# Rows and gates in two tables, ten gathers per expert, and a new order of the first expert's blocks

## The chip, the cores and the metric

The kernel runs on one core of a Trainium2 chip. The metric is the device time of one launch in microseconds (us); lower is better. The core's engines run side by side: TensorE (PE, matrix products), VectorE (DVE), ScalarE (ACT), GpSimd (POOL) and SyncE (SP, which issues transfers). They meet only at semaphores: an instruction waits until a counter has reached a value. POOL issues the indirect transfers (gathers and scatters), SP the plain ones.

## The reference

One transformer block with modulated layer norms, linear attention, and a mixture of eight experts, two per token. Cut to the part that the change touches:

```python
xf = x.reshape(-1, D)                       # N = 4096 tokens, D = 256
probs = softmax(xf @ router_w.T)            # E = 8 experts
topw, topi = top_k(probs, 2)                # normalised weights
# the best 640 tokens of each expert (capacity = 1.25 * N / E), by weight
disp = zeros((E, 641, D)).at[se, pos].set(xf[st])[:, :640]
g = einsum('ecd,edf->ecf', disp, wg)        # F = 1024
u = einsum('ecd,edf->ecf', disp, wu)
eo = einsum('ecf,efd->ecd', silu(g) * u, wd)
out = zeros_like(xf).at[st].add(eo[...] * weight)
y = x + gb * out                            # gb: one gate row per batch
```

## The kernel before

Attention comes first (to about 210 us); it leaves a table `h2_rows` in device memory. A row of it belongs to one token and holds 256 numbers that go into the experts, 256 gate numbers, and 8 expert weights: 520 numbers, 2080 bytes. Then the tokens of each expert are chosen by counting.

Each expert has 640 slots, five tiles of 128. `gather(e, par)` (POOL, L553) issues five indirect transfers, one per tile, each of which brings 128 whole rows into `xg[par]`. PE transposes the first 256 numbers of the tiles in three groups: tiles 0 and 1, tile 2, tiles 3 and 4 (`transpose_x(e, par, g)`, L1577; it waits for the group's gathers, `ga_d`). ACT casts each transposed group to `xT_h` (`x_high`, L711), DVE makes the rest `xT_l` (`x_low`, L1226), since every product is done in three passes of a high and a low part.

The hidden dimension is cut in eight blocks f. `gate_up(e, par, f)` (L1603) does two halves h of 320 slots; each half is 12 matmuls into two banks, six for the gate product (m=0) and six for the up product (m=1). Half h=0 needs the first two groups of tokens, half h=1 all three. After each half four steps follow: ACT `act_g` (silu, L729), DVE `hid` (product, L1258), ACT `hid_h` (L733), DVE `hid_l` (L1263). `down(e, f)` (L1624) takes both halves of `hid_h` and `hid_l` back through 15 matmuls into banks 4 to 6. PE's order is gate_up(f), down(f-1), so that the four steps hide behind one block. A half may overwrite its banks once `hid` of the half before has been formed (`hid_d`).

Weights: SP loads an expert's raw weights in two halves of the blocks (`load_weights`, L366; f below 4 is `raw_a`, the others `raw_b`); ACT casts them (`split_high`, L701) and DVE takes the rest (`split_low`, L1213), block by block, during the expert before. `raw_b` of expert e+1 is issued only when the first token group of e+1 has been transposed (`trx_d`, L449).

Beside this, DVE finds the tokens of the next expert: `describe_blocks`, `describe_facts`, `describe_rows` build tables of zeros and ones from the slots (`place_slots`, L1137); PE's `look(e)` (L1563) and DVE's `find_diagonal` (L1184), PE's `place(e)` (L1572) and DVE's `find_tokens` (L1193) give the indices `g_idx`, upon which POOL gathers. After its last `down` an expert's results are weighed (`weigh`, L1239, uses the gate numbers and weights in `xg`) and scattered with addition (`scatter`, L561).

The orders of all engines are written out by hand. For the first expert (e = 0) they differ: PE runs both halves of f=0, then both of f=1, with the third token group's transposes between the gate and the up product of the first half (L1620); `look(1)` stands ahead of `down(0, 0)`, `place(1)` in f=2. Expert 1's three token groups are transposed after gate_up of f=5, 6 and 7, while in the other experts it is f=4, 5 and 6 (`xf`, L1676). On DVE `place_slots(1)` stands ahead of the first `x_low`, and the description of expert 1 in block f=0.

Of the kernel before, what the change touches and what calls it, by code (L numbers as in the profile page):

```python
# [16 lines left out]
P = 128  # L17
F32, F32R = mybir.dt.float32, mybir.dt.float32r
BF16, I32, U32 = mybir.dt.bfloat16, mybir.dt.int32, mybir.dt.uint32
ALU = mybir.AluOpType  # L20
ACT = mybir.ActivationFunctionType
# [6 lines left out]
N = B * T  # L28
# [109 lines left out]
def build_program(nc, x, w_qkv, w_out, router, wg, wu, wd, c, wmod, rope, consts, out):  # L138
# [3 lines left out]
    h2_rows = nc.dram_tensor("h2_rows", (N, 2 * D + E), F32, kind="Internal").ap()  # L142
    h2_t = h2_rows[:, 0:D].rearrange("(n p) d -> n p d", p=P)
    gate_t = h2_rows[:, D:2 * D].rearrange("(b n p) d -> b p n d", b=B, p=P)
    w_t = h2_rows[:, 2 * D:].rearrange("(n p) e -> p n e", p=P)
# [3 lines left out]
    with ExitStack() as ctx:  # L149
# [3 lines left out]
        def sem(name):  # L153
            return ctx.enter_context(nc.semaphore(name))
# [189 lines left out]
        ga_d = [sem(f"ga_d{g}") for g in range(XG)]  # L344
# [120 lines left out]
        def _(pool):  # L465
# [87 lines left out]
            def gather(e, par):  # L553

                for a in range(CT):
                    nc.gpsimd.indirect_dma_start(  # L556
                        out=xg[par][:, a, :], out_offset=None, in_=h2_rows,
                        in_offset=bass.IndirectOffsetOnAxis(ap=g_idx[par][:, a:a + 1], axis=0))\
                        .then_inc(ga_d[next(g for g, t in enumerate(ROW_GROUPS) if a in t)], 16)

# [33 lines left out]
        def _(act):  # L594
# [123 lines left out]
            for g in range(XG):  # L718
                x_high(0, 0, g, bk=(0, 1, 7)[g])

            def expert(e, par, first=False):
                xf = FC - XG if first else XF
                for f in range(FC):
                    for h in range(2):
                        i = e * 2 * FC + 2 * f + h
                        wait(act, gu_d, i + 1)
                        if f or not first:
                            wait(act, hid_d, i - 1)
                        nc.scalar.activation(act_g[h][:, 0:HCAP], bank[2 * h][:, 0:HCAP], ACT.Silu).then_inc(silu_d, 1)  # L729
                        wait(act, hid_d, i + 1)  # L730
                        if f >= 2 or not first:
                            wait(act, dn_d, e * FC + f - 1)
                        nc.scalar.copy(hid_h[f % 2][:, h * HCAP:(h + 1) * HCAP], hid[h][:, 0:HCAP]).then_inc(hh_d, 1)  # L733
                    if xf <= f < xf + XG:
                        x_high(e + 1, 1 - par, f - xf)
                    if f < 2:

                        split_high(e, FC - 2 + f, e * FC + FC - 2 + f, implied=True)
                    else:
                        split_high(e + 1, f - 2, e * FC + FC + f - 2)  # L740
# [25 lines left out]
        def _(dve):  # L766
# [426 lines left out]
            def find_tokens(e, par):  # L1193

                dve.wait_ge(place_d, e + 1)
                TT(spot[:, :].rearrange("p (m q) -> p m q", q=Q),
                   bank[7][:, Q * BAND:(Q + 1) * BAND].rearrange("p (m q) -> p m q", q=Q),
                   own_q[:, :].unsqueeze(1).to_broadcast([P, BAND // Q, Q]), ALU.mult).then_inc(spot_d, 1)
                dve.wait_ge(spot_d, e + 1)
                with nc.allow_low_precision(reason="row numbers under 4096 are whole and exact"):  # L1200
                    RED(g_idx[par][:, :], spot[:, :].rearrange("p (v a q) -> p a v q", v=NV, q=Q), AXY, ALU.add)\  # L1201
                        .then_inc(idx_d, 1)
# [5 lines left out]
            def find_weights(e, par):  # L1208

                dve.wait_ge(trx_d, e * XG + XG)  # L1210
                V.tensor_copy(w_slot[par][:, :], xg[par][:, :, 2 * D + e]).then_inc(ws_d, 1)
# [21 lines left out]
            place_slots(1)  # L1233
            x_low(0, 0, 0, bk=0)
            x_low(0, 0, 1, bk=1)
            split_low(0, 4, 4)
            x_low(0, 0, 2, bk=7)
# [12 lines left out]

            def expert(e, par, first=False, ahead=True):

                def hidden(f, h):
                    i = e * 2 * FC + 2 * f + h
                    wait(dve, silu_d, i + 1)
                    if f or not first:
                        wait(dve, hh_d, i - 1)
                    V.tensor_tensor(hid[h][:, 0:HCAP], act_g[h][:, 0:HCAP], bank[2 * h + 1][:, 0:HCAP], ALU.mult)\  # L1258
                        .then_inc(hid_d, 1)
# [16 lines left out]
                xf = FC - XG if first else XF  # L1276
                for f in range(FC):
                    hidden(f, 0)
                    if f == 0 and first:
                        describe_blocks(1)  # L1280
                        describe_facts(1, 0)
                    if f == 0 and not first:
                        weigh(e - 1, 1 - par, 0, 2)
                    if f == (3 if first else 1):
                        find_tokens(e + 1, 1 - par)
# [6 lines left out]
                    if f == 0 and first:  # L1292
                        describe_facts(1, 1)
                        describe_rows(1, 0)
                        describe_rows(1, 1)
                    if f == 0 and not first:
                        weigh(e - 1, 1 - par, 2)
                    if f == 4:
                        find_weights(e, par)
                    hidden_low(f, 1)  # L1300
                    if f == 0 and first:
                        split_low(0, 5, 5)
# [6 lines left out]
                    if f == 1 and first:  # L1309
                        find_diagonal(1)  # L1310
# [15 lines left out]
            def last_expert(e, par):  # L1326

                for j in range(2 * FC):
# [9 lines left out]
                    if j == 4:  # L1338
                        find_weights(e, par)
                        dve.wait_ge(ws_d, e + 1)  # L1340
# [19 lines left out]
        def _(pe):  # L1360
# [242 lines left out]
            def gate_up(e, par, f, first=False):  # L1603
                W, XT = (w_h, w_l), (xT_h[par], xT_l[par])
                wait(pe, sp_l, e * FC + f + 1)
                for h in range(2):
                    if f == 0:
                        wait(pe, xl_d, e * XG + XG - 1 + h)
                    if f or not first:
                        wait(pe, hid_d, e * 2 * FC + 2 * f + h - 1)  # L1610
                    cols = slice(h * HCAP, (h + 1) * HCAP)
                    for m in range(2):
# [7 lines left out]
                        if first and (h, m) == (0, 0):  # L1620
                            transpose_x(0, 0, XG - 1, first=True)
                    last.then_inc(gu_d, 1)

            def down(e, f):  # L1624
                wait(pe, hh_d, e * 2 * FC + 2 * f + 2)
                wait(pe, hl_d, e * 2 * FC + 2 * f + 2)
# [48 lines left out]
            def expert(e, par, first=False, ahead=True, then_last=False):  # L1675
                xf = FC - XG if first else XF  # L1676
                for f in range(2, FC):
                    gate_up(e, par, f)
                    if f == 2 and first:
                        place(1)  # L1680
                    if xf <= f < xf + XG:
                        transpose_x(e + 1, 1 - par, f - xf)
                    down(e, f - 1)
                    if f == FC - 1 and ahead:
                        wait(pe, xl_d, e * XG + 2 * XG)
                        look(e + 2)
# [11 lines left out]
            gate_up(0, 0, 0, first=True)  # L1698
            gate_up(0, 0, 1)
            pe.wait_ge(idx_d, 1)  # L1700
            look(1)
            down(0, 0)
# [64 lines left out]
```

## Time and profile before

| | us |
|---|---|
| runs shown: median of 3 (lowest to highest) | 629.87 (627.71 to 632.21) |
| the profiled execution | 629.0 |
| its span, first to last instruction | 627.3 |
| PE busy | 583.7 (93%) |
| DVE busy | 452.5 (72%) |
| ACT busy | 320.4 (51%) |
| POOL busy | 269.8 (43%) |

The profiled execution took 629.0 us, of which 627.3 are the span that the trace shows and 1.7 lie around it. Attention fills the trace to about 210 us, the choice of tokens to about 246, the eight experts the rest. The mean granted clock of PE over the span was 0.993 of full speed. In the timelines a row is one instruction, or several alike ("x2"), with its start, its length, and in brackets the time that the engine stood idle before it and whom it had waited for. Matmuls overlap: one of 320 columns starts every 0.147 us or so though each is shown as 0.31 long, so lengths of a row of them are read from start to start.

### The profile page before, as it was taken

To read this page: it belongs to the slowest core of one execution; us is meant where nothing else is said; L and a number is where in the kernel's file an instruction comes from. 1 tells how busy PE (TensorE), PEld (TensorE's weight loads), DVE (VectorE), ACT (ScalarE), POOL (GpSimd) and SP (SyncE) were. 2 spreads that over 40 slices of the span, in tenths; PEclk is the share of its full clock that TensorE was granted. 3 is DMA by queue.
4 is the path that set the end of the run, shared out by engine and by line. 5 is a ranking of instruction groups with operands and counts; after the bars stand their busy time and mean duration, and the time that the engine had idled before them with its cause. 6 is when DMAs were issued, how large, how long until landed. Compare 5 with 4: busy or idle time off the path is not lost.

```text
span 627.3 us, 13151 instructions
## 1 busy us (share of the span) xinstructions
PE 583.7 (93%) x4013; PEld 527.4 (84%) x4013; DVE 452.5 (72%) x1357; ACT 320.4 (51%) x718; POOL 269.8 (43%) x406
## 2 busy tenths in 40 slices
PE   5999999999899778799899999999999999999993
PEld 4587779988787333599899999999999999999993
DVE  4688899998899888787567667666776775566441
ACT  4688878886444433244436445445444454354331
POOL 5788857776778302212061080170260440521321
PEclk9999999999999999899999999999999999999998
DMA  6322468644665730505356167066174373450312
GB/s 173 102 67 85 119 178 249 216 137 143 199 195 177 234 86 17 170 15 168 106 106 169 57 119 211 17 124 187 49 145 133 76 152 103 101 128 8 36 19 25
DMA packets 92482, 75.29 MB, mean 120 GB/s; under 512 B 12157, under 2 KB 89095, under 8 KB 92425
## 3 DMA queue, kind: packets, MB, share of 16 engines
q1 hardware_dynamic: 82344, 57.39, 30.7%
q0 software_dynamic: 8992, 15.90, 13.8%
q10 hardware_dynamic: 1088, 1.31, 0.7%
q8 instruction: 28, 0.46, 0.3%
q14 instruction: 30, 0.24, 0.1%
HBM read 52.41 MB, written 22.16 MB: 119 GB/s over the span
## 4 chain that ended last, share of the span: by engine, by line
PE 64%; DVE 9%; issue 4%; ACT 3%; DMA 3%; POOL 2%; SPq 1%; another core or an unknown queue 1%; POOLq 0%; ACTq 0%; DVEq 0%
PE bank L1617 29%; PE bank L1631 14%; PE bank L1652 4%; PE bank L1384 4%; PE bank L1509 4%; DVE hit L1075 2%; PE bank L1667 2%; PE bank L1495 2%; PE bank L1587 1%; PE bank L1421 1%; DMA q_in<-q_store 1%; DMA w_raw<-wd 1%; POOL xg L556 1%; PE bank L1464 1%
## 5 line engine op out<-in xcount | busy, mean ns | idle before, releaser
L556 POOL DMA_INDIRECT xg<-h_rows,g_idx x40 | 44.2, 1105 | 239.3 <-DVE g_idx L1201 229.5
L1617 PE MATMUL bank<-xT_h,w_h 128*128 128x320 f32 x448 | 140.5, 314 | 1.9 <-DVE hid L1258 0.9
L1617 PE MATMUL bank<-xT_l,w_h 128*128 128x320 f32 x448 | 138.6, 309 | 0.0
L1617 PE MATMUL bank<-xT_h,w_l 128*128 128x320 f32 x448 | 138.4, 309 | 0.0
L733 ACT CAST hid_h<-hid 128x320 fp32r<-128x320 f32 x112 | 51.5, 460 | 91.0 <-DVE hid L1258 83.6
L566 POOL DMA_INDIRECT out<-yo,s_idx x40 | 66.7, 1668 | 62.0 <-DVE yo L1323 26.6
L1617 PEld LDWEIGHTS bank<-xT_h,w_h 128*128 128x128 f32 x448 | 84.8, 189 | 3.6 <-issue 1.8
L729 ACT ACTIVATE act_g<-bank 128x320 f32<-128x320 f32 x112 | 48.9, 436 | 72.4 <-PE bank L1617 61.4
L1617 PEld LDWEIGHTS bank<-xT_l,w_h 128*128 128x128 f32 x448 | 84.7, 189 | 0.0
L1617 PEld LDWEIGHTS bank<-xT_h,w_l 128*128 128x128 f32 x448 | 84.6, 189 | 0.0
L1258 DVE TENSOR_TENSOR hid<-act_g,bank 128x320 f32<-128x320 f32 x112 | 54.2, 484 | 41.5 <-ACT act_g L729 38.2
L1263 DVE TENSOR_TENSOR hid_l<-hid,hid_h 128x320 fp32r<-128x320 f32 x112 | 54.8, 490 | 37.8 <-ACT hid_h L733 37.4
L1631 PE MATMUL bank<-w_h,hid_h 128*128 128x256 f32 x280 | 80.2, 286 | 0.0
L1631 PE MATMUL bank<-w_h,hid_l 128*128 128x256 f32 x280 | 78.3, 280 | 0.3 <-issue 0.3
L1631 PE MATMUL bank<-w_l,hid_h 128*128 128x256 f32 x280 | 78.3, 280 | 0.0
L1216 DVE TENSOR_TENSOR w_l<-w_raw,w_h 128x768 fp32r<-128x768 f32 x64 | 61.1, 960 | 11.4 <-ACT w_h L706 10.9
L706 ACT CAST w_h<-w_raw 128x768 fp32r<-128x768 f32 x64 | 52.8, 832 | 2.5 <-DMA w_raw<-wd 2.5
L1631 PEld LDWEIGHTS bank<-w_h,hid_l 128*128 128x128 f32 x280 | 52.8, 189 | 0.6 <-issue 0.5
L1631 PEld LDWEIGHTS bank<-w_l,hid_h 128*128 128x128 f32 x280 | 52.8, 189 | 0.2
L1384 PE MATMUL bank<-wqkv_h,hT_h 128*128 128x256 f32 (+1 forms) x128 | 49.2, 384 | 4.1 <-DVE hT_l L968 2.5
L1631 PEld LDWEIGHTS bank<-w_h,hid_h 128*128 128x128 f32 x280 | 52.7, 188 | 0.1
L542 POOL TENSOR_TENSOR rot<-rot_a,rot_b 128x512 f32<-128x512 f32 x32 | 42.3, 1321 | 11.3 <-DVE rot_b L961 10.7
(225 smaller groups left out, 1330.1 us busy)
## 6 DMA issues: line engine op xcount, KB each, us to landing
w_raw<-wg SPq DMA_DIRECT2D x32, 256.0 KB, 3.4
w_raw<-wu SPq DMA_DIRECT2D x32, 256.0 KB, 4.8
w_raw<-wd SPq DMA_DIRECT2D x16, 512.0 KB, 5.8
x_in<-x SPq DMA_DIRECT2D x32, 128.0 KB, 2.2
q_store<-qT SPq DMA_DIRECT2D x32, 128.0 KB, 2.2
q_in<-q_store SPq DMA_DIRECT2D x32, 128.0 KB, 2.3
x_re<-x SPq DMA_DIRECT2D x32, 128.0 KB, 2.1
out<-x SPq DMA_DIRECT2D x32, 128.0 KB, 2.1
```

The costliest lines, as they stand in the source:

```text
L542: nc.gpsimd.tensor_tensor(rot[s.par(0)][:, :], rot_a[:, :], rot_b[:, :], ALU.add).then_inc(rope_d, 1)
L556: nc.gpsimd.indirect_dma_start(out=xg[par][:, a, :], out_offset=None, in_=h2_rows, in_offset=bass.IndirectOffsetOnAxis(ap=g_idx[par][:, a: ...
L566: nc.gpsimd.indirect_dma_start(out=out_rows, out_offset=bass.IndirectOffsetOnAxis(ap=s_idx[par][:, a:a + 1], axis=0), in_=yo[:, a, :], in_ ...
L706: nc.scalar.copy(w_h[:, f, :], w_raw[:, f, :]).then_inc(sp_h, 1)
L729: nc.scalar.activation(act_g[h][:, 0:HCAP], bank[2 * h][:, 0:HCAP], ACT.Silu).then_inc(silu_d, 1)
L733: nc.scalar.copy(hid_h[f % 2][:, h * HCAP:(h + 1) * HCAP], hid[h][:, 0:HCAP]).then_inc(hh_d, 1)
L1216: V.tensor_tensor(w_l[:, f, :], w_raw[:, f, :], w_h[:, f, :].bitcast(F32), ALU.subtract).then_inc(sp_l, 1)
L1258: V.tensor_tensor(hid[h][:, 0:HCAP], act_g[h][:, 0:HCAP], bank[2 * h + 1][:, 0:HCAP], ALU.mult)\
L1263: V.tensor_tensor(hid_l[f % 2][:, h * HCAP:(h + 1) * HCAP], hid[h][:, 0:HCAP], hid_h[f % 2][:, h * HCAP:(h + 1) * HCAP].bitcast(F32), ALU. ...
L1384: ins = MM(out, x[j][:, k, :], w[i][:, k, cols], start=n == 0, stop=n == 3 * KC - 1)
L1617: last = MM(bank[2 * h + m][:, 0:HCAP], W[i][:, f, at:at + P], XT[j][:, k, cols], start=n == 0, stop=n == 3 * KC - 1)
L1631: last = MM(bank[4 + a // 2][:, a % 2 * D:(a % 2 + 1) * D], (hid_h, hid_l)[j][f % 2][:, a * P:(a + 1) * P], (w_h, w_l)[i][:, f, 4 * P:], s ...
```

## The change

1. The table is split: `h2_rows` keeps the 256 token numbers (1024 bytes a row), a new `g_rows` takes gates and weights (1056 bytes a row).
2. `gather` issues ten transfers: five for the token rows, which count `ga_d` as before, then five for gates and weights, which count a new `ga_rest`. `find_tokens(e)` waits until the gathers of all experts before e have landed whole; `find_weights` loses its wait.
3. The first expert opens in another order of half-blocks: (f=0, h=0), (f=1, h=0), (f=0, h=1), (f=1, h=1). The third token group is transposed in the middle of the second of them. `down(0, 0)` waits for three pieces.
4. ACT's and DVE's orders for the opening follow: DVE does two `x_low` ahead of `place_slots(1)`, and the description of expert 1 is spread between the steps; the splits of the expert's last four weight blocks come behind it.
5. In expert 0 `look(1)` moves from ahead of `down(0, 0)` to behind gate_up of f=2, `place(1)` to f=3, `find_tokens(1)` from the first to the second half of f=3 on DVE, `find_diagonal(1)` from f=1 to f=2. Expert 1's token groups are transposed at f=4, 5, 6, behind `down(f-1)` and not ahead of it.

```diff
-    h2_rows = nc.dram_tensor("h2_rows", (N, 2 * D + E), F32, kind="Internal").ap()
+    h2_rows = nc.dram_tensor("h2_rows", (N, D), F32, kind="Internal").ap()
+    g_rows = nc.dram_tensor("g_rows", (N, D + E), F32, kind="Internal").ap()
...
                 for a in range(CT):
                     nc.gpsimd.indirect_dma_start(
-                        out=xg[par][:, a, :], out_offset=None, in_=h2_rows,
+                        out=xg[par][:, a, 0:D], out_offset=None, in_=h2_rows,
...
+                for a in range(CT):
+                    nc.gpsimd.indirect_dma_start(
+                        out=xg[par][:, a, D:], out_offset=None, in_=g_rows,
+                        in_offset=bass.IndirectOffsetOnAxis(ap=g_idx[par][:, a:a + 1], axis=0)).then_inc(ga_rest, 16)
...   ACT
-            for g in range(XG):
-                x_high(0, 0, g, bk=(0, 1, 7)[g])
+            x_high(0, 0, 0, bk=0)
+            x_high(0, 0, 1, bk=1)
+            opening_silu(0)
+            x_high(0, 0, 2, bk=7)
+            opening_high(0)
+            opening_silu(1)
+            opening_high(1)
+            split_high(0, FC - 2, FC - 2, implied=True)
+            opening_silu(2)
+            opening_high(2)
+            opening_silu(3)
+            opening_high(3)
+            split_high(0, FC - 1, FC - 1, implied=True)
...   DVE
             def find_tokens(e, par):
+                wait(dve, ga_rest, e * CT * 16)
                 dve.wait_ge(place_d, e + 1)
...
             def find_weights(e, par):
-                dve.wait_ge(trx_d, e * XG + XG)
...
-            place_slots(1)
             x_low(0, 0, 0, bk=0)
             x_low(0, 0, 1, bk=1)
-            split_low(0, 4, 4)
-            x_low(0, 0, 2, bk=7)
+            place_slots(1)
...
+            opening(0)
+            describe_blocks(1)
+            x_low(0, 0, 2, bk=7)
+            opening_low(0)
+            opening(1)
+            describe_facts(1, 0)
+            opening_low(1)
+            opening(2)
+            opening_low(2)
+            opening(3)
+            opening_low(3)
+            describe_facts(1, 1)
+            describe_rows(1, 0)
+            describe_rows(1, 1)
+            split_low(0, 4, 4)
+            split_low(0, 5, 5)
...   PE
+            def opening(j):
+                f, h = j % 2, j // 2
+                pe.wait_ge(sp_l, f + 1)
+                pe.wait_ge(xl_d, XG - 1 + h)
+                if j >= 2:
+                    pe.wait_ge(hid_d, j - 1)
+                for m in range(2):
...
+                    if (j, m) == (1, 0):
+                        transpose_x(0, 0, XG - 1, first=True)
...
             def expert(e, par, first=False, ahead=True, then_last=False):
-                xf = FC - XG if first else XF
+                xf = XF
                 for f in range(2, FC):
                     gate_up(e, par, f)
                     if f == 2 and first:
+                        pe.wait_ge(idx_d, 1)
+                        look(1)
+                    if f == 3 and first:
                         place(1)
-                    if xf <= f < xf + XG:
+                    if xf <= f < xf + XG and not first:
                         transpose_x(e + 1, 1 - par, f - xf)
                     down(e, f - 1)
+                    if xf <= f < xf + XG and first:
+                        transpose_x(e + 1, 1 - par, f - xf)
...
-            gate_up(0, 0, 0, first=True)
-            gate_up(0, 0, 1)
-            pe.wait_ge(idx_d, 1)
-            look(1)
-            down(0, 0)
+            for j in range(4):
+                opening(j)
+            down(0, 0, pieces=3)
             expert(0, 0, first=True)
```

## Rows read from the trace of the kernel before

**Rows 1.** Timeline of PE, first expert: start us, us, instruction, idle before and releaser
```profile
254.49 0.44 PE L1587 MATMUL bank<-const_sb,xg 128*128 128x128 f32 x2 [0.73 <-DMA xg<-h_rows,g_idx]
...
255.94 0.39 PE L1617 MATMUL bank<-xT_h,w_h 128*128 128x320 f32 x1 [0.36 <-DVE xT_l L1230]
...
258.51 0.66 PE L1587 MATMUL bank<-const_sb,xg 128*128 128x128 f32 x4 [1.45 <-DMA xg<-h_rows,g_idx]
...
260.57 0.64 PE L1617 MATMUL bank<-xT_h,w_h 128*128 128x320 f32 x1 [0.52 <-DVE xT_l L1230]
...
263.92 0.31 PE L1617 MATMUL bank<-xT_h,w_h 128*128 128x320 f32 x1
...
273.94 0.19 PE L1575 MATMUL bank<-diag,same_r 128*128 128x40 bf16 x1 [0.45 <-DVE diag L1191]
...
305.37 0.73 PE L1568 MATMUL bank<-facts,onehot 128*128 128x160 bf16 x8 [1.94 <-DVE xT_l L1230]
305.89 0.39 PE L1617 MATMUL bank<-xT_h,w_h 128*128 128x320 f32 x1
```

**Rows 2.** Busy time by window: window, us, engines' busy us, granted clock, DMA share, GB/s
```profile
262.00:264.00 2.00, 2.00 (x10) 2.00 (x9) 1.32 (x3) 0.00 (x0) 0.00 (x0) 0.53 0.82 236
```

**Rows 3.** The chain that ended last, first expert: start us, us, what
```profile
275.99 3.51 PE bank L1617 x24
279.51 1.73 PE bank L1631 x15
...
289.99 0.45 PE bank L1587 x4
```

**Rows 4.** Timeline of ACT, columns as for PE
```profile
254.97 0.37 ACT L715 CAST xT_h<-bank 128x256 fp32r<-128x256 f32 x1 [0.79 <-PE bank L1587]
...
299.98 0.83 ACT L706 CAST w_h<-w_raw 128x768 fp32r<-128x768 f32 x1 [2.49 <-DMA w_raw<-wd]
```

**Rows 5.** Timeline of POOL, gathers of experts 0 and 1
```profile
250.72 1.42 POOL L556 DMA_INDIRECT xg<-h_rows,g_idx  x1 [0.30 <-issue]
...
253.69 1.13 POOL L556 DMA_INDIRECT xg<-h_rows,g_idx  x1 [0.30 <-issue]
279.36 1.28 POOL L556 DMA_INDIRECT xg<-h_rows,g_idx  x1 [24.53 <-DVE g_idx L1201]
```

**Rows 6.** Timeline of DVE, opening and description of expert 1
```profile
254.77 1.02 DVE L1230 TENSOR_TENSOR xT_l<-bank,xT_h 128x512 fp32r<-128x512 f32 x2
...
260.96 0.17 DVE L1155 TENSOR_SCALAR block_no<-slot 128x32 int32<-128x32 int32 x1
...
262.10 0.82 DVE L1167 TENSOR_TENSOR facts<-vals,in_block 128x640 bf16<-128x640 bf16 x1
...
265.73 1.29 DVE L1175 TENSOR_TENSOR onehot<-iota_s,row_in 128x512 bf16<-128x512 bf16 x2
...
267.33 1.82 DVE L1216 TENSOR_TENSOR w_l<-w_raw,w_h 128x768 fp32r<-128x768 f32 x2
...
273.11 0.32 DVE L1187 TENSOR_TENSOR band<-bank,own_q 128x160 f32<-128x160 f32 x1
...
278.90 0.20 DVE L1201 TENSOR_REDUCE g_idx<-spot 128x5 int32<-128x40 f32 x1
```

**Rows 7.** The page's costliest groups: line, operation, count | busy us, mean ns | idle before
```profile
L1263 DVE TENSOR_TENSOR hid_l<-hid,hid_h 128x320 fp32r<-128x320 f32 x112 | 54.8, 490 | 37.8 <-ACT hid_h L733 37.4
```

**Rows 8.** Timeline of SP's queue, the load of expert 2's second half
```profile
331.84 0.93 SPq L377 DMA_DIRECT2D w_raw<-wg  x2
```

**Rows 9.** Timeline of POOL in expert 1: the last transfer of its scatter
```profile
330.35 2.29 POOL L566 DMA_INDIRECT out<-yo,s_idx  x1 [0.30 <-issue]
```

**Rows 10.** Timeline of ACT in expert 1: the cast that needs that load
```profile
344.28 0.83 ACT L706 CAST w_h<-w_raw 128x768 fp32r<-128x768 f32 x1
```

**Rows 11.** Busy time by window, quiet ahead of the gathers and behind that load
```profile
226.00:228.00 2.00, 1.54 (x9) 0.59 (x7) 1.78 (x13) 0.60 (x2) 0.00 (x0) 1.00 0.00 0
...
339.00:340.00 1.00, 1.00 (x9) 1.00 (x8) 0.81 (x3) 0.76 (x2) 0.00 (x0) 1.00 0.19 62
```

## What the change does to the time: the prediction

> **What bounds the kernel now.** I read the page's busy times first: PE is busy for 93% of the span, so a change counts only where it takes idle or slow time out of PE's path, or puts some in. Then the chain that ended last: from the first expert on it is almost all PE, gate_up and down in turn, a block of 3.51 us and a down of 1.73 [rows 3]. Then the waits of PE: in experts 1 to 6 it hardly stops, so the change can win only in the opening and in expert 0, which it reorders. There the timeline shows where PE stood [rows 1]: 1.45 us for the gathers of the third token group, 0.52 for its `x_low`, 0.45 for the diagonal of expert 1, and 1.94 at the end for the last `x_low` of expert 1. In between ran 12 matmuls at half clock: from 260.57 to 263.92 they took 3.35 us where half a block takes 1.76, 1.6 too many; the granted clock of 262 to 264 reads 0.53 [rows 2], that is 1.2 GHz, after PE had done little from 257 to 260.5 [rows 1]. The 1.94 has a cause further back: the load of expert 1's second weight half is issued behind the transposes that end at 290.44 [rows 3], its data end ACT's 2.49 us wait at 299.98 [rows 4], and the last `x_low` stands behind all that.
>
> Accounting: the first opening matmul starts at 255.94, that of expert 1 at 305.89 [rows 1], 49.95 us. The work in it is 8 blocks and 7 downs, 40.2, three groups of four transposes and one of two (0.45 and 0.22), 1.6, two looks of 0.52 and a place of 0.1, 1.1: together 42.9. The other 7.05 us are stops and slow clock. What the change is worth is how much of them it leaves.
>
> **The change, walked through.** I lay the new orders on the durations of before, in the clock of its trace.
>
> Start. The second `x_low` ended at 255.79 [rows 6], since `place_slots` (1.6 us) ran ahead of it. Now it follows its cast, which ended at 255.34 [rows 4], by about 0.42: PE starts at 255.8 if the rows land as before. They should land sooner, since each gather brings half the bytes. The third gather's issue ended at 252.14 and its transposes began 2.35 us later; the fifth ended at 254.82 and its began 3.69 later [rows 1, 5]: the last wait behind the bytes of the others. With 1024 of 2080 bytes the 2.35 lies between 1.16 (all of it goes with the bytes) and 2.35 (none does); halfway gives 0.6 less, but the matmuls between the transposes hide some. I take 255.6, bounds 255.3 and 255.8. The Trainium skill, "DMA: Bandwidth & Descriptors" (Anatomy of one DMA), gives a fixed 2.0 us and bytes over 436 GB/s for such a transfer. By that estimate a gather of 128 rows goes from 2.6 to 2.3 us, and the start would be 255.5. The third gather's 2.35 agrees with the size of it.
>
> First two half-blocks. From 255.6 half (0, 0) runs to 257.36, the gate product of (1, 0) to 258.24. The last token rows should have landed at 254.82 + 2.35 = 257.2, at worst at 258.51 as before: no wait, at worst 0.3. Transposes 0.45, up product 0.88: 259.6. So the 1.45 goes.
>
> Third half. In before it was 2.06 us from the start of those transposes to the matmul that needs them (258.51 to 260.57 [rows 1]). Now from 258.24: 260.3, and 0.05 for `describe_blocks` (1.14 us, 260.96 to 262.10 [rows 6]), which DVE runs just ahead of that `x_low`. PE waits 0.75 us, in place of 0.52. But it has been at work since 255.6 with no other gap, so I let the clock stay at full speed. Two halves to 263.85.
>
> `down(0, 0)` needs three pieces through all four steps. The third half ends at 262.1; four steps of 0.49 at most [rows 7] and their hand-overs make 2.1, and ACT's cast of weight block 6 may add 0.1: 264.35, a new wait of 0.5. In before `look(1)` and block 1 hid it. Then down to 266.1, block 2 to 269.6, look 270.1, down(1) 271.85, block 3 275.35.
>
> Diagonal. DVE now carries more ahead of `find_diagonal(1)`. The fourth half ends at 263.85, and its low part is done on DVE at 265.9. Behind it follow a half of the facts (0.74), both rows (1.20) and two splits (1.74), each read from start to start, 0.08 less than its row [rows 6]: 269.6. Then product 0.41, split 0.87, `describe_blocks(2)` 1.14, low part and product 0.82: 272.8; a cast on ACT to wait for, 0.5, low part 0.4, two splits 1.74: 275.5. From the diagonal's first instruction to `place` it was 0.83 [rows 1, 6]: 276.35. PE comes to `place(1)` at 275.35 and waits 1.0, in place of 0.45; behind it in PE's queue stand down(2) and all later blocks. That is the change's largest new cost.
>
> Expert 1's gather. place, down(2), block 4, down(3): 283.5. DVE needs product, facts, targets, low part and product (2.05 us) from 276.25 before `find_tokens`, 0.43: indices at 278.75. POOL starts 0.26 later (279.10 to 279.36 [rows 5, 6]), two gathers take 1.28, 0.30 and 1.13: 281.7. With 1.2 to 2.35 for landing the first group is there between 282.9 and 284.1, PE asks at 283.5: a wait of 0 to 0.6, I take 0.3.
>
> The rest. From 283.8 four transposes, block 5, down(4), two transposes, block 6, down(5), four transposes, block 7, down(6) and look: 17.35, which gives 301.15 for expert 1's first matmul. The load of the second weight half goes out at 284.3, 6 us sooner; counted with the same 9.4 us that it took before (to 299.98, beside another load) it is there at 293.7, and ACT's cast of it is due behind block 6 at about 295. So the 2.49 and the 1.94 go, also because the last `x_low` now stands in f=6.
>
> **What costs nothing.** Stores into two tables: they move the same bytes, and the transfers are quiet from 226 [rows 11], 20 us before the first gather; without that cover the gathers would wait for them. The waits on `ga_rest` are for gathers of the expert before, issued most of a block sequence earlier. Five more POOL issues of 1.13 + 0.30 [rows 5] are 7.1 us an expert. Behind them stand the five scatters, and for these waits `weigh`, seven blocks of 5.24 us, 36 us, later. The gate rows are needed there too.
>
> **Sum.** 305.89 - 301.15 = 4.7 us: 0.3 at the start, and 7.05 us of stops cut to some 2.6 (0.75, 0.5, 1.0, 0.3). On the profiled execution's 629.0 (627.3 of span and 1.7 around it) this gives 624.3. That execution was 0.9 under the median of the runs, 629.87, from which it would be 625.2. I predict 624.7. Bounds: all the small costs at their worse ends (start 0.2, gather 0.3, transposes 0.3) leave 3.9; all new waits at nothing give 7.2, but the diagonal's 1.0 is a sum of DVE's own work and hardly goes.
>
> **Rivals.**
> - The clock falls all the same. PE has gaps at 254 to 255.6 and at 259.6; if it falls there, 12 matmuls again cost 1.6. For it speaks that in before a wait of similar size stood in just this stretch [rows 1, 2]; against it, that the 1.45 before it is gone. With rows that land no sooner, the gain is 2.3 to 3.1: 626.5. Chance 0.18.
> - More is won: the rows land fast enough to bring the start to 255.3, the wait for expert 1's rows is none, and DVE overtakes part of the diagonal's delay. Gain 5.5 to 7: 622.7. Chance 0.14.
> - Slower: scatters run into the weight loads. In expert 1 the last scatter's issue ends at 332.64 [rows 9], and the load of expert 2's second half is issued at 331.84 [rows 8], so the two hardly meet. With 7.1 us more of gathers all of the scatter's second half runs beside the load, in each of six experts. The load is over by 339.8 [rows 11] and its cast starts at 344.28 [rows 10], 4.5 us of cover; then cast, low part and product (2.2 us) must be ready for PE's next expert, which comes one block and one down after block 6, about 4 us more. So it decides once the load is 8 us longer, twice its length; beyond that each us is paid six times. At 2 us each the gain turns into 12 - 4.7 = 7.3 us of loss: 636.3. The Trainium skill, "DMA: Bandwidth & Descriptors" (Rules for kernel authors), would have many small transfers coalesced into one large, which speaks against ten gathers in place of five. The cover in these rows is why I give it little. Chance 0.06.
>
> **How the numbers follow.** The forecast has 0.62 (gain 3.5 to 5.5, so 623.5 to 626.4 from the one base or the other). The range takes in the clock's case and most of the better one: 621.9 to 627.6, and leaves out some 0.15. A measurement of this kernel, whose runs spread from 627.71 to 632.21, can tell about 1%, 6.3 us, from no change. Faster by more than that needs a gain over 6.3: the better case's upper half and chance in the runs, 0.16. Slower over 1%: 0.05. Within: 0.79.
>
> **What would show it.** Of the new profile: gathers of experts show ten POOL issues with the first group's transposes after shorter landings; the granted clock from 260 to 264 at 1.0; PE's waits in expert 0 are `x_low` 0.75, `hid_l` 0.5 ahead of the first down, `diag` 1.0, rows of expert 1 up to 0.6, and no 1.94 at the end; expert 1's first matmul near 301; ACT waits for no weights at f=6. A clock at half speed, a longer `diag` or row wait, or PE waiting for `hid` in experts 1 to 6 behind late weights would make it wrong.

## The result, and the profile after

The changed kernel is slower: 659.6 us (median of 6 runs, 657.79 to 673.03) against 628.49 for the kernel before on the same chip, a ratio of 1.049 (95% interval 1.0455 to 1.0526). Ratios, here and below, are of fast executions alone: those over 1.5% above the fastest of the same kernel (here the one of 673.03) are in the medians but not in the ratios. The profiled execution took 658.09 us, its span 656.2. The forecast was 624.7, with 627.6 as its upper end.

First the page's busy times and PE's granted clock:

```profile
PE 597.5 (91%) x4013; PEld 535.8 (82%) x4013; DVE 453.3 (69%) x1357; ACT 320.9 (49%) x718; POOL 310.0 (47%) x446
...
PEclk9999999999999999999979989989999989979999
```

POOL has the 40 transfers more that the change gives it, and 40 us of work more. PE's work is the same 4013 matmuls but 13.8 us longer: in the second half the granted clock dips five times, in experts 1, 2, 3, 5 and 6. Its slices read 7 or 8 there, where before they stood at 9 until the end.

Then each expert's length, from its first gate activation on ACT's timeline to the next expert's: before, experts 0 to 6 took 47.9, 44.3, 44.4, 44.4, 44.4, 43.8, 45.5 us; after, 48.3, 52.5, 49.9, 50.0, 48.4, 48.5, 50.9. Experts 1 to 6 lost 33.6 us. All else together won 4.6: the way from the first gather to expert 1's first activation 2.15 (61.16 to 59.01), the last expert 1.0, the end of the program 2.2; only the first gather came 0.8 later.

What stands in those experts? Busy time by window, for one expert of before and the same of after (us, busy us of PE, PEld, DVE, ACT, POOL with their instructions, granted clock, DMA share, GB/s):

```profile
352.30:396.70 44.40, 44.24 (x333) 43.94 (x332) 30.66 (x61) 21.09 (x44) 13.81 (x10) 1.00 0.50 117
```

```profile
359.13:409.03 49.90, 46.38 (x333) 45.43 (x332) 30.84 (x61) 21.31 (x43) 18.98 (x15) 0.97 0.43 104
```

Of 5.5 us more, 3.4 are idle time of PE (3.52 after, 0.16 before) and 2.1 go to the same matmuls, at a lower clock. The DMA engines are less busy than before, so they are not the bound. The timeline of that stretch shows the stop itself:

```profile
369.31 0.31 PE L1690 MATMUL bank<-xT_h,w_l 128*128 128x320 f32 x1
...
369.65 0.44 ACT L757 ACTIVATE act_g<-bank 128x320 f32<-128x320 f32 x1 [0.98 <-PE bank L1690]
...
372.94 0.83 ACT L711 CAST w_h<-w_raw 128x768 fp32r<-128x768 f32 x1
...
374.01 1.57 POOL L562 DMA_INDIRECT xg<-g_rows,g_idx  x1 [0.31 <-issue]
...
374.55 0.31 PE L1690 MATMUL bank<-xT_h,w_l 128*128 128x320 f32 x1
...
379.00 0.44 ACT L757 ACTIVATE act_g<-bank 128x320 f32<-128x320 f32 x1 [5.24 <-remote]
379.47 0.49 DVE L1314 TENSOR_TENSOR hid<-act_g,bank 128x320 f32<-128x320 f32 x1 [4.72 <-ACT act_g L757]
...
380.02 0.42 PE L1690 MATMUL bank<-xT_h,w_h 128*128 128x320 f32 x1 [1.67 <-issue]
...
381.84 0.32 PE L1690 MATMUL bank<-xT_h,w_h 128*128 128x320 f32 x1 [0.24 <-issue]
...
382.56 0.41 PE L1690 MATMUL bank<-xT_h,w_l 128*128 128x320 f32 x1 [0.24 <-issue]
```

The matmul at 374.55 is the last of a half-block. It ends by the profile at 374.86, and the silu that needs only this half starts at 379.00, 4.1 us late. One block earlier the hand-over took 0.03: the matmul ends at 369.62, the silu starts at 369.65. The trace's list of semaphore rises has this rise at 378.98, while those of ACT and DVE in the same stretch stand 0.01 behind their instructions. So PE's completion is told late, ACT and DVE stand, and at 380.02 PE runs out of finished hidden parts. The end of a matmul is modelled, so the trace alone does not show whether the work itself was late or only the word of it; the 27 matmuls behind this one, to 378.07, start at their usual distance. From 381.3 PE itself only creeps, a pair of matmuls and then a hole. In expert 1 the same creeping goes on for 7 us: the matmuls of a `down`, which wait for nothing that the profile shows ("issue"), start in ones and twos some 0.7 us apart.

```profile
325.55 0.28 PE L1702 MATMUL bank<-w_l,hid_h 128*128 128x256 f32 x1 [1.11 <-issue]
325.67 0.28 PE L1702 MATMUL bank<-w_h,hid_h 128*128 128x256 f32 x1
326.27 0.28 PE L1702 MATMUL bank<-w_h,hid_l 128*128 128x256 f32 x1 [0.33 <-issue]
326.39 0.28 PE L1702 MATMUL bank<-w_l,hid_h 128*128 128x256 f32 x1
326.99 0.37 PE L1702 MATMUL bank<-w_h,hid_h 128*128 128x256 f32 x1 [0.33 <-issue]
```

The busy times of the creeping and of what follows it, at half clock:

```profile
324.00:331.30 7.30, 3.38 (x17) 2.22 (x15) 0.35 (x1) 0.00 (x0) 5.82 (x5) 0.90 0.42 91
331.30:337.00 5.70, 4.65 (x18) 4.65 (x19) 3.15 (x7) 2.86 (x6) 4.79 (x4) 0.53 0.64 73
```

In the view of waits many of these late hand-overs are put down to "remote", since no instruction ends near them. First the kernel before, then the changed one (engine, what waits, releaser: us in total, times, longest; from 300 us on):

```profile
ACT act_g L729 <- remote: 9.5, 3, 5.1
```

```profile
ACT act_g L757 <- remote: 40.1, 11, 8.0
```

The kernel before has three of that name, each while its five gathers or the scatters behind ran; this is the longest:

```profile
549.08 0.44 ACT L729 ACTIVATE act_g<-bank 128x320 f32<-128x320 f32 x1 [5.06 <-remote]
```

PE did not wait for them, and so they were in none of the rows that the prediction was built on. The view does not name them all. If a hand-over is called late where the silu starts more than 0.6 us behind both the last matmul's end and ACT's own work before it, the timelines have ten in the kernel before, up to 4.0 us, and twenty in the changed one, up to 8.0 us.

### The profile page after: what moved, and what is told of

The parts are those of the page before. It is cut to its first block, busy times and chain, and to the rows that moved or that the text cites. A ratio compares the mean times of both kernels' runs of the same rounds, so it can differ in the third digit from the quotient of the medians.

```text
span 656.2 us, 13200 instructions
## 1 busy us (share of the span) xinstructions
PE 597.5 (91%) x4013; PEld 535.8 (82%) x4013; DVE 453.3 (69%) x1357; ACT 320.9 (49%) x718; POOL 310.0 (47%) x446
## 4 chain that ended last, share of the span: by engine, by line
PE 60%; DVE 11%; issue 9%; ACT 3%; DMA 2%; POOL 1%; another core or an unknown queue 0%; POOLq 0%; SPq 0%; DVEq 0%; ACTq 0%
PE bank L1690 27%; PE bank L1702 13%; PE bank L1723 4%; PE bank L1563 4%; PE bank L1438 2%; DVE hit L1102 2%; PE bank L1738 2%; PE bank L1641 1%; PE bank L1549 1%; DMA x_in<-x 1%; PE bank L1670 1%; DVE hid L1314 1%; PE bank L1475 1%; DVE w_l L1243 1%; PE bank L1573 1%
## 5 line engine op out<-in xcount | busy, mean ns | idle before, releaser
L1690 PE MATMUL bank<-xT_h,w_h 128*128 128x320 f32 x432 | 139.1, 322 | 17.3 <-DVE hid L1314 10.1
L1690 PE MATMUL bank<-xT_h,w_l 128*128 128x320 f32 x432 | 136.4, 316 | 0.8 <-issue 0.8
L1690 PE MATMUL bank<-xT_l,w_h 128*128 128x320 f32 x432 | 136.6, 316 | 0.1
L1314 DVE TENSOR_TENSOR hid<-act_g,bank 128x320 f32<-128x320 f32 x108 | 52.3, 485 | 72.9 <-ACT act_g L757 49.9
L757 ACT ACTIVATE act_g<-bank 128x320 f32<-128x320 f32 x108 | 47.2, 437 | 105.0 <-PE bank L1690 59.9
L760 ACT CAST hid_h<-hid 128x320 fp32r<-128x320 f32 x108 | 49.6, 460 | 87.2 <-DVE hid L1314 78.9
L571 POOL DMA_INDIRECT out<-yo,s_idx x40 | 64.1, 1604 | 59.2 <-DVE yo L1376 25.7
L1319 DVE TENSOR_TENSOR hid_l<-hid,hid_h 128x320 fp32r<-128x320 f32 x108 | 52.9, 490 | 36.1 <-ACT hid_h L760 33.3
L1702 PEld LDWEIGHTS bank<-w_h,hid_h 128*128 128x128 f32 x280 | 53.1, 190 | 1.7 <-issue 1.0
L562 POOL DMA_INDIRECT xg<-g_rows,g_idx x40 | 43.3, 1082 | 12.2 <-issue 12.2
```

Of the source, the lines that this page charges most:

```text
L562: nc.gpsimd.indirect_dma_start(out=xg[par][:, a, D:], out_offset=None, in_=g_rows, in_offset=bass.IndirectOffsetOnAxis(ap=g_idx[par][:, a: ...
L571: nc.gpsimd.indirect_dma_start(out=out_rows, out_offset=bass.IndirectOffsetOnAxis(ap=s_idx[par][:, a:a + 1], axis=0), in_=yo[:, a, :], in_ ...
L1319: V.tensor_tensor(hid_l[f % 2][:, h * HCAP:(h + 1) * HCAP], hid[h][:, 0:HCAP], hid_h[f % 2][:, h * HCAP:(h + 1) * HCAP].bitcast(F32), ALU. ...
L1690: last = MM(bank[2 * h + m][:, 0:HCAP], W[i][:, f, at:at + P], XT[j][:, k, cols], start=n == 0, stop=n == 3 * KC - 1)
L1702: last = MM(bank[4 + a // 2][:, a % 2 * D:(a % 2 + 1) * D], (hid_h, hid_l)[j][f % 2][:, a * P:(a + 1) * P], (w_h, w_l)[i][:, f, 4 * P:], s ...
```

## Experiments: which part, which place, which distance

Fifteen kernels, in order. "Ratio" is that of the runs to those of the kernel before on the same chip, with its 95% interval (the median is that of all runs; the kernel before had 626.0 to 628.5 on the chips used); an expert's length is taken as above, from the profiled execution.

| run | median us | ratio | expert 0 | experts 1 to 5, mean |
|---|---|---|---|---|
| kernel before | 628.49 | | 47.9 | 44.3 |
| changed kernel | 659.6 | 1.049 (1.0455 to 1.0526) | 48.3 | 49.9 |
| e1_order_only | 625.49 | 0.998 (0.9954 to 0.9998) | 46.3 | 44.1 |
| e2_tables_only | 638.5 | 1.020 (1.0157 to 1.0236) | 46.7 | 45.8 |
| e3_gates_last | 625.93 | 0.998 (0.9953 to 1.0012) | 53.1 | 44.1 |
| e4_gates_late | 625.2 | 0.996 (0.993 to 0.9987) | 49.6 | 44.0 |
| e5_paced | 618.45 | 0.984 (0.9804 to 0.988) | 46.0 | 43.9 |
| e6_tiny_rest | 674.11 | 1.071 (1.0662 to 1.0762) | 56.0 | 51.5 |
| e7_ten_late | 669.15 | 1.065 (1.061 to 1.0694) | 56.1 | 51.1 |
| e8_spread | 621.68 | 0.990 (0.9871 to 0.9932) | 45.8 | 44.4 |
| f1_before_paced | 623.75 | 0.992 (0.9893 to 0.9942) | 45.9 | 43.9 |
| f2_order_paced | 621.93 | 0.991 (0.988 to 0.9932) | 46.4 | 43.9 |
| f3_short_pace | 684.91 | 1.093 (1.0886 to 1.0975) | 56.1 | 53.6 |
| f4_tiny_paced | 618.73 | 0.986 (0.9827 to 0.9886) | 46.4 | 43.9 |
| g1_pace_256 | 618.46 | 0.991 (0.9868 to 0.9942) | 45.7 | 44.0 |
| g2_pace_128 | 637.24 | 1.003 (0.9986 to 1.0077) | 45.7 | 45.6 |
| g3_one_pause | 618.67 | 0.989 (0.9853 to 0.992) | 45.8 | 44.0 |

**Which part.** Two runs take the change apart; in them theory A is the ten gathers, theory B the new order. `e1_order_only` keeps the new order and goes back to one table and five gathers.

```diff
-    h2_rows = nc.dram_tensor("h2_rows", (N, D), F32, kind="Internal").ap()
-    g_rows = nc.dram_tensor("g_rows", (N, D + E), F32, kind="Internal").ap()
+    h2_rows = nc.dram_tensor("h2_rows", (N, 2 * D + E), F32, kind="Internal").ap()
...
-                        out=xg[par][:, a, D:], out_offset=None, in_=g_rows,
```

> The new order of the first expert's blocks with one table and five whole-row gathers per expert. If the ten gathers are what costs the 30 us (theory A), the stalls of 5 to 8 us in experts 1 to 6 go, the period of an expert is 44 to 45 us again, and the time is 625 to 629 us. If the new order shifts the phase of something else (theory B), they stay and the time is 650 to 660 us. If both are needed, it lies between, 632 to 648 us.

`e2_tables_only` is the kernel before with the two tables and the ten gathers:

```diff
-                        out=xg[par][:, a, :], out_offset=None, in_=h2_rows,
+                        out=xg[par][:, a, 0:D], out_offset=None, in_=h2_rows,
...
+                        out=xg[par][:, a, D:], out_offset=None, in_=g_rows,
```

> The kernel before with two tables and ten gathers per expert, rows first, its order of blocks kept. Theory A: the stalls of ScalarE at the gate activation are there in each of experts 1 to 6 and the time is 652 to 664 us. Theory B: no more than the two short stalls of before, and 626 to 631 us.

The order alone costs nothing (625.49), the gathers alone cost 12.5 us (638.5). So it is the gathers, and together with the new order they cost more than alone: why the 12.5 became 31 was not taken apart further. What the trace of e2 shows is that it too has late hand-overs in each of experts 1 to 6, but its clock falls to half only once there, in expert 6 (0.51 from 554 to 564 us; that expert takes 52.8 us, against 45.5 before). The second number missed theory A's 652.

**Which place.** Two runs leave the number of gathers and move the five for gates: behind the scatters,

```diff
             def expert(e, par):
...
                 gather(e + 1, 1 - par)
                 scatter(e - 1, 1 - par)
+                gather_rest(e + 1, 1 - par)
```

> The changed kernel with the five gate gathers of an expert issued behind the five scatters instead of ahead of them, in one unbroken run as before. If the number of indirect transfers in one run counts (theory A1), the stall stays, 650 to 662 us, and begins at the same count of transfers. If gathers are worse than scatters (A2), it moves behind the scatters and may fall where PE has something to do; the stall at the third block is gone.

and there with a wait for DVE's count of hidden parts ahead of it (`wait_apart(pool, hid_d, e * 2 * FC + 10, apart)`).

> As the run with the gates last, but the five gate gathers wait until the hidden parts of the fifth block of the expert are made, so that GpSimd issues ten transfers, pauses some 8 to 10 us, and issues five. If an unbroken run of fifteen is the cause (A1), the stalls go and the time is 624 to 632 us. If each transfer more costs its share wherever it stands (A3), the stall moves and the time stays at 645 us or more.

Both bring experts 1 to 5 back to 44 us. In e3 POOL issues the same fifteen transfers without a pause, so neither their number (A3) nor the length of the unbroken run (A1) is the cause by itself. But e3's expert 0, where ten gathers still follow one another twice, takes 53.1. A scatter starts 1.9 us behind the one before it, a gather 1.25. So I formed another theory, called B in the runs from here on: gathers that close together pile something up, PE's completions wait in it, and slower transfers let it drain.

**Which distance.** `e5_paced` leaves all ten in one run in their place, with a fill of a spare tile behind each (the wait before the fill is for the fill before).

```diff
+            def breathe(n):
+                wait_apart(pool, pace_d, n, apart)
+                nc.gpsimd.memset(pace[:, :], 0.0).then_inc(pace_d, 1)
...
                         .then_inc(ga_d[next(g for g, t in enumerate(ROW_GROUPS) if a in t)], 16)
+                    breathe(e * 2 * CT + a)
```

> The changed kernel with all ten gathers in one run ahead of the scatters, where they were, but GpSimd fills a spare tile (0.53 us) behind each gather, so that they start about 1.9 us apart, as the scatters do, and not 1.25. If the short distance between gathers lets a backlog grow in which TensorE's completions wait (theory B), experts 1 to 6 take 44 to 45 us each again and the time is 622 to 633 us. If the number of transfers ahead of the scatters counts (theory C), or blocks 2 to 5 are a bad place for the gate gathers (theory P), the experts take 48 to 50 us and the time is 648 us or more.

618.45 us, 1.6% under the kernel before and under the forecast too, with no late hand-over left; PE runs without a hole at full clock:

```profile
349.00:393.00 44.00, 44.00 (x334) 43.90 (x333) 31.38 (x61) 21.50 (x44) 24.97 (x25) 1.00 0.46 118
```

The timeline of POOL shows that 1.66 us, less than I had expected, is distance enough:

```profile
322.78 0.95 POOL L569 DMA_INDIRECT xg<-g_rows,g_idx  x1 [0.17 <-POOL pace L558]
323.74 0.54 POOL L558 MEMSET pace<- 128x512 f32 x1
324.44 0.95 POOL L569 DMA_INDIRECT xg<-g_rows,g_idx  x1 [0.16 <-POOL pace L558]
```

`e6_tiny_rest` cuts the tables so that the second five gathers bring only the eight weights (`w_rows`, `(N, E)`), 32 bytes a row.

> The changed kernel with the tables cut elsewhere: the first holds row and gate (2 KB), the second only the eight weights of a token (32 bytes), so the second five gathers move almost nothing, and still follow 1.25 us apart. The bytes in all are the same. If it is transfers issued (B or C), the stalls stay: experts of 47 to 50 us, 640 to 660 us. If it is the bytes that the second five move, they go: 622 to 630 us.

`e7_ten_late` puts five idle gathers behind e3's gate gathers (`gather_spare`, into a tile that nobody reads), so that ten follow one another in the second half of an expert.

> The run with the gates last (five row gathers, five scatters, five gate gathers, 44.1 us per expert) and behind them five gathers more, of the gates into a tile that nobody reads: ten gathers 1.25 us apart again, but in the second half of an expert, behind the scatters. Theory B: the stall is back, in the late blocks, 47 to 50 us per expert and 640 to 660 us. If only the place counted (P): 44 to 45 us per expert, 624 to 630 us.

`e8_spread` is e3 with the gate gathers of experts 0 and 1 held back in the opening as well (`pool.wait_ge(hid_d, 4)` and `pool.wait_ge(hid_d, 14)`).

> The run with the gates last, and in expert 0 the gate gathers held back too: those of expert 0 until its second block's first half is made, those of expert 1 until the seventh block's. Theory B: expert 0 takes 46 to 48 us instead of 53.1, the others keep 44.1, and the time is 618 to 623 us, under that of the run with the gates last by 3 to 7 us. If the first expert is lost to something else, 624 to 628 us.

Fewer bytes in the second five gathers are no cure: with those nearly empty the time is 674.11. This is not the price of empty gathers alone, since e6's first five bring 2 KB a row in place of 1. The place is not the cause either: ten close together in late blocks cost 7 us per expert again (51.1 against e3's 44.1, with five transfers more). The sizes were over what I had expected of both, and of e6's I have no account. e8 brings expert 0 from 53.1 to 45.8, a little better than forecast; its later experts take 44.4, not 44.1.

**Is it the distance?** `f3_short_pace` has e5's instructions with a fill of 32 columns (`pace = sb("pace", [P, 32])`):

> The paced run with ten gathers, but the fill is of 32 columns and not 512: the same instructions and semaphores on GpSimd, about 0.1 us instead of 0.53, so the gathers stay nearly as close as without (1.25 to 1.35 us). If it is the distance that cures (theory B), the stalls are back and the time is 640 to 660 us. If an instruction or a semaphore between two gathers is enough, 617 to 622 us.

```profile
322.87 0.14 POOL L558 MEMSET pace<- 128x32 f32 x1
323.17 0.95 POOL L563 DMA_INDIRECT xg<-h_rows,g_idx  x1 [0.17 <-POOL pace L558]
324.13 0.14 POOL L558 MEMSET pace<- 128x32 f32 x1
324.43 1.46 POOL L563 DMA_INDIRECT xg<-h_rows,g_idx  x1 [0.17 <-POOL pace L558]
```

The gathers are 1.25 us apart again, and the time is 684.91, the worst of all and far over the forecast. An instruction between them cures nothing; the time between them does. Why it is 25 us worse than the changed kernel at the same distance is open. `f4_tiny_paced` gives e6's empty gathers e5's fill:

> The run whose second five gathers move 32 bytes a row (674 us), with the fill of 0.53 us behind each of the ten. If the distance between transfers decides and not what they move, the stalls go here too: 617 to 624 us. If small transfers have a harm of their own, 630 us or more.

618.73: spread out, it does not matter what they move. The fill alone, in the kernel before (f1) and with the new order on one table (f2):

> The kernel before (one table, its order of blocks) with the spare fill of 0.53 us behind each of its five gathers. Theory B says that five gathers 1.25 us apart already delay TensorE's completions a little in each expert, hidden but for some 0.5 us (44.3 to 44.4 us per expert against 43.8 in the paced run): experts of 43.8 us and a time 2 to 5 us under the kernel before. If five gathers cost nothing, no change.

> The new order of the first expert's blocks with one table and five gathers, paced in the same way. If the tables have no worth of their own, 617 to 621 us, as the paced run with ten gathers (618.5). If the short row gathers are worth the 1 to 2 us that the prediction gave them, 619 to 622 us. The difference to the kernel before with the pace is the worth of the new order: 3 to 5 us by the prediction's sum.

Pacing five gathers already gives 0.8% (f1), though PE hardly waited there. By the count above, e5, f1, f2 and f4, all with the long fill, have no late hand-over at all. The new order adds 1.8 us (f2 against f1), under the 3 to 5 of the forecast, the tables 3.5 (e5 against f2, on another chip); in the profiled spans 3.1 of the 3.2 between these two lie in the last expert and the end.

**Distance or pile.** Two fills between, of 256 and 128 columns, and one pause: g3 has no fill between gathers but eight in a row ahead of the sixth.

> The paced run with ten gathers and a fill of 256 columns, about 0.33 us: gathers some 1.45 us apart. If the loss falls by degrees with the distance, about half of it is left: 635 to 655 us. If there is a step between 1.25 and 1.45, 617 to 623 us; if it lies above 1.45, 660 us or more.

> The same with 128 columns, about 0.23 us: gathers some 1.35 us apart. By degrees: 650 to 675 us. Step between 1.25 and 1.35: 617 to 623 us.

> The changed kernel with no fill between gathers (1.25 us apart) but eight fills, 5 us in all, between an expert's fifth gather and its sixth. If a pile decides that a pause clears (theory B): the experts take 44 to 45 us, 622 to 630 us. If each distance counts by itself: the stalls stay, 645 us or more.

At 1.45 us apart nothing is lost (618.46), though twelve late hand-overs of up to 3.0 us are back under PE's cover; at 1.34 apart the median is 637.24, between the two forecasts, and the runs spread from 625.85 to 647.09, so that the ratio in the table, from the four lowest of ten, shows only its better side; at 1.25 apart 659.6. And with one pause of 6 us, every other distance at 1.25, 618.67, under the forecast (seven late hand-overs, up to 3.2 us, hidden too). So theory B's pile fits: it grows over more than five gathers at the short distance, and a pause clears it. Seven of the runs (e5, e8, f1, f2, f4, g1, g3) are under the kernel before by 0.8 to 1.6%, their intervals wholly under 1; e1 and e4 are so by 0.2 and 0.4%.

**What stays open** is what piles up. The weight loads are not it: they keep the DMA engines far busier, PE runs full beside them, and no hand-over is late in the load shown. Busy time of before, in the gathers and in a load:

```profile
316.00:322.00 6.00, 6.00 (x48) 6.00 (x47) 3.69 (x8) 2.09 (x4) 4.74 (x5) 1.00 0.53 137
333.00:339.00 6.00, 6.00 (x47) 5.99 (x46) 4.99 (x11) 3.73 (x9) 0.00 (x0) 1.00 0.97 272
```

Nor is it the fetching of instructions: in the stop of the changed kernel, 369 to 381.5, the DMA view lists one queue alone, that of the gathers and scatters, while the page has queues of kind "instruction" beside it.

```profile
q0 software_dynamic: 438, 1.22, 34.5%
```

It could also be the recording. Each run here lists a span and a granted clock, so none was without it. The Trainium skill, "NOTIFIC — the notification-queue block" (7.1 Overflow: three behaviours, one of which stalls the engine), says that the block that takes the engines' records holds its producers back rather than lose one inside, and that its count of stalls, if not zero, would mean that it had throttled an engine. No run here reads that count, nor shows how the kernel does without records.

## Why the prediction was wrong, point by point

**The step that failed** is "Five more POOL issues of 1.13 + 0.30 [rows 5] are 7.1 us an expert" under what costs nothing. The issues did take that little (1.08 us each in the mean, and 0.30), and `weigh` never waited. But the step asked only who waits for the gathers, and not what ten of them so close do to the engines beside them. With it failed what the prediction drew from PE hardly stopping in experts 1 to 6: that held for the kernel before, but in the changed one PE stood 3.5 us in the expert shown and took 2.1 longer over its matmuls, part of them at half clock. Rows of before showed the sign: a silu that waits 5.1 us for matmuls long done, in the waits of ACT. The prediction used PE's waits alone.

**The slower rival** had the right sign and the wrong mechanism. ACT waits for no weight load anywhere in the changed kernel, its view of waits has no `w_raw` at all (before had one such wait, the 2.49 of expert 0 [rows 4]); with the gathers spread or paced the transfers are as many and the time is under before. The rule quoted beside it, from the Trainium skill, "DMA: Bandwidth & Descriptors" (Rules for kernel authors), to coalesce small transfers, spoke against this change and is borne out by the changed kernel, but not by the paced ones: ten gathers (618.45) lose nothing against five (621.93).

**The opening** went as forecast in most points. PE's rows that answer to [rows 1], first of the changed kernel, then of the paced one (e5):

```profile
256.26 0.39 PE L1670 MATMUL bank<-xT_h,w_h 128*128 128x320 f32 x1 [0.37 <-DVE xT_l L1257]
262.39 0.39 PE L1670 MATMUL bank<-xT_h,w_h 128*128 128x320 f32 x1 [1.94 <-issue]
266.55 0.36 PE L1702 MATMUL bank<-w_h,hid_h 128*128 128x256 f32 x1 [0.40 <-DVE hid_l L1288]
278.46 0.19 PE L1629 MATMUL bank<-diag,same_r 128*128 128x40 bf16 x1 [0.54 <-DVE diag L1218]
...
304.50 0.40 PE L1690 MATMUL bank<-xT_h,w_h 128*128 128x320 f32 x1
```

```profile
256.79 0.39 PE L1678 MATMUL bank<-xT_h,w_h 128*128 128x320 f32 x1 [0.37 <-DVE xT_l L1265]
261.83 0.38 PE L1678 MATMUL bank<-xT_h,w_h 128*128 128x320 f32 x1 [0.84 <-issue]
265.98 0.35 PE L1710 MATMUL bank<-w_h,hid_h 128*128 128x256 f32 x1 [0.40 <-issue]
277.90 0.19 PE L1637 MATMUL bank<-diag,same_r 128*128 128x40 bf16 x1 [0.56 <-DVE diag L1226]
...
302.73 0.40 PE L1698 MATMUL bank<-xT_h,w_h 128*128 128x320 f32 x1
```

- Start: forecast 0.3 sooner. From POOL's first gather it was 9.08 us before (246.86 to 255.94) and 8.64 after (247.62 to 256.26): 0.44.
- The 1.45 for the third group: gone in both. The clock drop of [rows 2]: gone, 262 to 264 reads 1.00.
- The third half's `x_low`, forecast 0.75: 1.94 in the changed kernel, where gate gathers ran from 255.73 on, and 0.84 paced. The 1.1 between them is a late hand-over too: the transposes end at 259.58 and ACT's cast of them starts at 260.98; paced it is 260.10 and 260.14.
- `down(0, 0)`, forecast 0.5: 0.40 in both. The diagonal, forecast 1.0: 0.54, so DVE was quicker than my walk. Rows of expert 1, 0 to 0.6: no wait. The 1.94 at the end: gone.
- Expert 1's first matmul, forecast 4.7 sooner. From the first gather it was 59.03 us before, 56.88 after and 54.51 paced: 2.15 in the changed kernel, which lost 1.1 more at the third half and the rest in ways not taken apart, and 4.5 paced. But the kernel before with the pace alone has it at 56.65 (247.80 to 304.45). So of the 4.5 only 2.1 belong to the change, and 2.4 are the pace's; the agreement with 4.7 is partly chance.

**The end** I had not looked at. From the last scatter's issue to the end of the span it is 5.8 us in the kernels with one table (before, e1, f1, f2) and 3.3 to 3.6 in those with two, but for e7 (two tables and a spare gather) with 5.6. The view of SP's waits, before and after, puts 2.4 of it on PE's closing hand-over; what in the program makes the difference was not looked for.

```profile
SPq L149 <- PEq L149: 3.4, 1, 3.4
```

```profile
SPq L150 <- PEq L150: 1.0, 1, 1.0
```

With the pace on both sides the whole change is worth 623.75 to 618.45, 0.8% by the ratios (0.9918 and 0.9842), about the forecast's size. That is luck in good part: 2.1 us of it are the opening and expert 0, for which the forecast had 4.7, and 2.4 the end, which it did not have.

## What to carry to other kernels

When a change gives an engine more small transfers in a row, look past that engine: does a hand-over elsewhere already wait for work that is done? In the view of waits such a wait often has no releaser among the engines ("remote"), and it may be hidden from the bound. Where it is there, spread the transfers before making more of them: here a pause, or 0.2 us more between them, was worth 40 us in a kernel that otherwise lost 31. And price an edit on the paced kernel too: it shows the edit's own worth.

## What the runs showed of the hardware that I had not expected

- Ten indirect gathers 1.25 us apart made PE's completions up to 8.0 us late and PE's own issue creep; 1.45 us apart they cost no time, and a pause of 6 us behind the fifth cleared it. Five in a row already cost about 0.4 us per expert (44.3 in the kernel before, 43.9 in f1).
- Taking the bytes out of the second five gathers (32 a row) did not help at the short distance: 674.11 us, with first five of 2 KB a row, against 659.6.
- The harm does not go with the load on the DMA engines: PE ran full at a DMA share of 0.97 (333 to 339 of before) and crept at 0.42 (324 to 331.3 of the changed kernel).
